# Forward sums of a graph layer as two float32r matmuls, with the message split by ScalarE and VectorE

## The reference, cut to what matters

```
proj = einsum('ni,rio->rno', feat, W)          # 16 relations
m    = proj[etypes, src_idx] + bias
m    = m * (1 / in_degree)[dst_idx][:, None]
out  = segment_sum(m, dst_idx, num_segments=n) # 53125 edges
```

## Time and profile before

| | |
|---|---|
| three runs | 2062.16, 2066.46, 2066.49 us, median 2066.46 |
| profiled execution | span of 2062.0 us from first to last instruction; the lowest run is 0.2 us above it |
| TensorE busy | 1966.0 us, 95% |
| VectorE busy | 1150.2 us, 56% |
| ScalarE busy | 607.9 us, 29% |
| GpSimd busy | 993.8 us, 48% |
| chain that ended last | TensorE 84%, VectorE 5%, DMA 5%, ScalarE 3% |
| line 690, both projections | 733.1 us in 1600 records, two for each matmul |
| line 772, sums of both directions | 486.5 us in 1760 records, two for each matmul |
| line 808, additions | 371.0 us in 880 |
| line 745, gathers | 831.5 us in 832 |

### The profile page before, as it was taken

How to read it: one execution, slowest core, us unless ns; L and a number is a source line. 1 busy time by engine, 2 the same in 40 slices (tenths; PEclk the granted TensorE clock), 3 DMA queues, 4 the chain that set the end, 5 groups by cost and what they waited for, 6 DMA issues and landing times.

```text
span 2062.0 us, 27476 instructions
## 1 busy us (share of the span) xinstructions
PE 1966.0 (95%) x8235; PEld 1360.8 (66%) x8235; DVE 1150.2 (56%) x2484; ACT 607.9 (29%) x1262; POOL 993.8 (48%) x966
## 2 busy tenths in 40 slices
PE   7999999999999999999998889999999499999998
PEld 3446544456666666555565566888888488888897
DVE  4999991056666666444787668555558711111111
ACT  2332333322222222222433222222223722222243
POOL 0000001067777777777567777777762023333332
PEclk9999999999999999999999999999997699999999
DMA  8332235456666656666555454333332754544573
GB/s 293 156 143 98 108 153 229 173 182 196 190 185 191 191 188 193 208 212 206 183 159 175 142 159 139 103 101 102 97 95 82 264 166 113 130 112 122 131 197 73
DMA packets 134186, 326.97 MB, mean 159 GB/s; under 512 B 24576, under 2 KB 65184, under 8 KB 132768
## 3 DMA queue, kind: packets, MB, share of 16 engines
q1 hardware_dynamic: 80064, 199.64, 26.7%
q0 software_dynamic: 50688, 123.79, 23.6%
q10 hardware_dynamic: 3296, 1.80, 0.3%
HBM read 196.42 MB, written 128.71 MB: 158 GB/s over the span
## 4 chain that ended last, share of the span: by engine, by line
PE 84%; DVE 5%; DMA 5%; ACT 3%; issue 2%; POOL 1%; DVEq 0%; POOLq 0%
PE bank L690 31%; PE bank L772 16%; PE bank L1983 10%; PE bank L1994 9%; PE bank L1912 4%; PE bank L1903 4%; DMA arena<-table_bwd,arena 3%; PE bank L597 3%; PE bank L1841 1%; DVE arena L808 1%; POOL arena L745 1%; DVE arena L409 1%; DMA table_fwd<-arena 1%; PE bank L1952 1%; ACT arena L1710 1%
## 5 line engine op out<-in xcount | busy, mean ns | idle before, releaser
L690 PE MATMUL bank<-arena,work 128*128 128x512 f32 x1600 | 733.1, 594 | 2.5 <-ACT arena L683 1.5
L808 DVE TENSOR_TENSOR arena<-arena,bank 128x257 f32 x880 | 371.0, 422 | 370.9 <-PE bank L772 298.8
L772 PE MATMUL bank<-arena 128*128 x1760 | 486.5, 388 | 24.3 <-DMA arena<-table_bwd,arena 15.9
L745 POOL DMA_INDIRECT arena<-table_fwd,arena x416 | 419.9, 1009 | 144.7 <-issue 86.0
L745 POOL DMA_INDIRECT arena<-table_bwd,arena x416 | 411.6, 989 | 152.4 <-issue 81.7
L690 PEld LDWEIGHTS bank<-arena,work 128*128 128x128 f32 x1600 | 299.3, 190 | 278.7 <-issue 261.8
L683 ACT ACTIVATE arena<-bank 128x512 f32<-128x512 f32 x400 | 239.6, 599 | 702.8 <-PE bank L690 699.2
L772 PEld LDWEIGHTS bank<-arena 128*128 128x128 f32 x1760 | 317.1, 191 | 144.0 <-issue 110.0
L1053 POOL DMA_INDIRECT out<-xn,work x56 | 89.5, 1599 | 249.7 <-DVE xn L193 181.7
L754 DVE TENSOR_TENSOR arena<-cst,arena 128x512 f32<-128x512 f32 x220 | 151.5, 689 | 97.9 <-PE bank L690 97.9
L1727 ACT ACTIVATE arena<-bank,work 128x256 f32<-128x256 f32 (+1 forms) x280 | 120.8, 432 | 284.2 <-PE bank L1983 277.6
(11 more groups left out here) (323 smaller groups left out, 1589.5 us busy)
## 6 DMA issues: line engine op xcount, KB each, us to landing
table_fwd<-arena SPq DMA_DIRECT2D x100, 512.0 KB, 2.6
table_bwd<-arena SPq DMA_DIRECT2D x100, 512.0 KB, 3.2
arena<-in_W SPq DMA_DIRECT2D x35, 1024.0 KB, 5.7
arena<-in_W SPq DMA_DIRECT2D x2, 4096.0 KB, 13.9
arena<-table_fwd,arena POOLq DMA_INDIRECT x416, 3.1
arena<-table_bwd,arena POOLq DMA_INDIRECT x416, 2.8
work<-x_transposed SPq DMA_DIRECT2D x50, 128.0 KB, 3.6
mix_rows<-arena SPq DMA_DIRECT2D x25, 256.0 KB, 2.6
```

Source lines behind the costliest of these rows:

```text
L690: last = pe.matmul(ps[4 + s % 2][:, :], xT[t % 2][:, k * P:(k + 1) * P], ar(W_off[d] + k * 4096 + c * 512, 512), start=(k == 0), stop=(k = ...
L745: e.indirect_dma_start(msg[m % RING][:, 0:C], None, table[d], bass.IndirectOffsetOnAxis(ap=idx[d][:, j:j + 1], axis=0)).then_inc(s_ga[m % ...
L772: pe.matmul(ps[sum_bank(n)][:, 0:W], oh[n % OHS], msg_all[:, ds(place.pop(n), W)], start=True, stop=True).then_inc(s_sm, 1)
L808: vec.tensor_tensor(to, to, ps[sum_bank(n)][:, 0:W], ALU.add).then_inc(s_ac, 1)
```

## The change

Each of the 416 forward sums beside the second projection becomes two matmuls in the type float32r. ScalarE copies the message into `hi` (which rounds it to float32r), VectorE subtracts, `lo = message - hi`, and TensorE multiplies the one-hot by `hi` (258 columns, two of them ones) and then by `lo` (256 columns) into the same PSUM bank. There are six buffers for each half. ScalarE works up to four sums ahead of TensorE's slot, VectorE up to two ahead. The 24 forward sums behind the projection and all backward sums stay as they are.

The forward sums now begin at slot 4, not slot 2, and end at slot 197. The halves lie over tiles 12 to 24 of `X1`, so SyncE loads these rows of x again once the last such sum is done, and the first addition to tile 12 waits for that. The one-hots have a tensor of their own. Some semaphores are merged, since new ones are needed. TensorE no longer reads the message's address into registers for these sums; ScalarE and VectorE each do, four addresses at a time.

```diff
+        oh = [onehot[:, j * P:(j + 1) * P] for j in range(OHS)]
+        hi = [half_t[:, j * (C + 2):(j + 1) * (C + 2)] for j in range(HB)]
+        lo = [half_t[:, HB * (C + 2) + j * C:HB * (C + 2) + (j + 1) * C] for j in range(HB)]
...
-            pe.matmul(ps[sum_bank(n)][:, 0:W], oh[n % OHS], msg_all[:, ds(place.pop(n), W)],
-                      start=True, stop=True).then_inc(s_sm, 1)
+            if n in rank:
+                i = rank[n]
+                e.wait_ge(s_lo, i + 1)
+                pe.matmul(ps[sum_bank(n)][:, 0:C + 2], oh[n % OHS], hi[i % HB], start=True, stop=False)
+                pe.matmul(ps[sum_bank(n)][:, 0:C], oh[n % OHS], lo[i % HB], start=False, stop=True).then_inc(s_sm, 1)
+            else:
+                pe.matmul(ps[sum_bank(n)][:, 0:W], oh[n % OHS].bitcast(f32), msg_all[:, ds(place.pop(n), W)],
+                          start=True, stop=True).then_inc(s_sm, 1)
...
+        def high_half(e, n):
+            i = rank[n]
+            if n % 4 == 0:
+                load_halves(act, high_at, n)
+            e.wait_ge(s_ga[n % GS], 16 * (n // GS + 1))
+            if i >= HB:
+                e.wait_ge(s_sm, split[i - HB] + 1)
+            act.activation(hi[i % HB][:, 0:C], msg_all[:, ds(high_at.pop(n), C)], ACT.Copy).then_inc(s_hi, 1)
+        def low_half(e, n):
+            i = rank[n]
+            if n % 4 == 0:
+                load_halves(vec, low_at, n)
+            e.wait_ge(s_hi, i + 1)
+            vec.tensor_tensor(lo[i % HB], msg_all[:, ds(low_at.pop(n), C)], hi[i % HB][:, 0:C],
+                              ALU.subtract).then_inc(s_lo, 1)
...
-            return min(TE - LEFT, max(0, (s - 2) * (TE - LEFT) // (SLOTS - 4)))
+            return min(TE - LEFT, max(0, (s - 4) * (TE - LEFT) // (SLOTS - 6)))
+        def halves_upto(s, ahead):
+            return min(TE - LEFT, forward_upto(s + 1) + ahead) if s >= 4 else 0
+        split = list(range(TE - LEFT))
+        rank = {n: i for i, n in enumerate(split)}
...
+                e.wait_ge(s_sm, split[-1] + 1)
+                e.dma_start(X1[:, XT * C:NT * C].rearrange("p (t c) -> p t c", c=C),
+                            a["x"][XT * P:NT * P, :].rearrange("(t p) c -> p t c", p=P)).then_inc(ldx_again, 16)
...
+                    for n in range(halves_upto(s - 1, 2), halves_upto(s, 2)):
+                        if n in rank:
+                            low_half(e, n)
                     add_sums(e, forward_upto(s), forward_upto(s + 1))
...
                     evacuate(SLOTS + s)
                     late_sort_copies(s)
+                    for n in range(halves_upto(s - 1, 4), halves_upto(s, 4)):
+                        if n in rank:
+                            high_half(e, n)
```

More of the change, by code:

```diff
@@ L28 @@
                             mybir.dt.float16)
+f32r = mybir.dt.float32r
 ALU, ACT, AX = mybir.AluOpType, mybir.ActivationFunctionType, mybir.AxisListType
@@ L138, in end_of_block @@
             nc.all_engine_barrier()
-        arena = sb("arena", 36232)
+        arena = sb("arena", ARENA)
+        with nc.sbuf_tensor("x_lead", [P, XL], f32), nc.sbuf_tensor("halves", [P, HB * (2 * C + 2)], f32r) as half_t:
+            pass
         X1 = sb("X1", NT * C)
+        onehot = sb("onehot", OHS * P, f32r)
         xn = sb("xn", NT * C)
@@ L373, in build @@
         W_off = [R2, R1]
-        ld, lde, ldf, ldh, ldr, zbd = (sem(n) for n in
-            ("ld_const", "ld_edges", "ld_fold", "ld_half", "ld_rows", "zero"))
+        ld, lde, ldf, zbd = (sem(n) for n in
+            ("ld_const", "ld_edges", "ld_fold", "zero"))
         ldx = sems("ld_x", 3)
         XG = ((0, 5), (5, 15), (15, NT))
-        ldw, s_wb = sems("forward_weights", 4), sem("backward_weights")
+        ldw, s_wb = sems("forward_weights", 4), sem("weights_in")
         folded, s_pmo = sem("folded"), sem("fold_out")
@@ L724, in build @@
         msg_ones = ar(R2, RING * W).rearrange("p (j w) -> p j w", w=W)[:, :, C]
-        oh = [ar(R2 + RING * W + j * P, P) for j in range(OHS)]
+        oh = [onehot[:, j * P:(j + 1) * P] for j in range(OHS)]
+        hi = [half_t[:, j * (C + 2):(j + 1) * (C + 2)] for j in range(HB)]
+        hi_ones = half_t[:, 0:HB * (C + 2)].rearrange("p (j w) -> p j w", w=C + 2)[:, :, C:C + 2]
+        lo = [half_t[:, HB * (C + 2) + j * C:HB * (C + 2) + (j + 1) * C] for j in range(HB)]
         msg_all = ar(R2, RING * W)
@@ L789, in load_places, with load_halves @@
             place.update((n + i, v) for i, v in enumerate(at))
+        high_at, low_at = {}, {}
+        def load_halves(eng, at, n):
+            _, v = nc.values_load_multi_w_load_instructions(
+                placei[0][0:1, n:n + 4], engines=(eng.engine,), min_val=0, max_val=(RING - 1) * W,
+                skip_runtime_bounds_check_because="edge_places takes the tile modulo RING before it multiplies by W")
+            at.update((n + i, x) for i, x in enumerate(v) if n + i in rank)
+        def high_half(e, n):
[13 more added lines that the diff above has]
+                              ALU.subtract).then_inc(s_lo, 1)
         def load_columns(n):
@@ L1088, in _ @@
                 e.dma_start(ei[2], a["et"]).then_inc(lde, 16)
-                e.dma_start(so_f.hcst, a["half"]).then_inc(ldh, 16)
+                e.dma_start(so_f.hcst, a["half"]).then_inc(lde, 16)
                 for t in range(NT):
```

55 lines of the change are left out of this document (30 added, 25 removed).

## The result

The changed kernel takes 2095.72 us (median of four executions), the one before 2065.45 beside it: 1.015 times as long, 95% interval 1.0136 to 1.0163, some 30 us. One of the four took 3965.35 us, no trace of it is kept and the ratio leaves it out; the other three lie between 2091.96 and 2097.74, with 2093.70 in the middle. The profiled execution agrees, with a span of 2091.7 us against 2062.0. The forecast was 2075. Its direction was right. The change is between three and four times as large as forecast: inside the range of 8 in 10 (2052 to 2105), outside the forecast's own range (2067 to 2092).

What follows compares the result with a forecast made beforehand. TensorE was taken as the bound, GpSimd and VectorE close behind. Losing 7.3 us in the sort (VectorE) and 0.8 behind it (GpSimd) makes 8 us, so 2075 us; own range 2067 to 2092, 8 in 10 from 2052 to 2105.

Steps and rivals of the forecast that it cites:

- The bound moves to VectorE in the sort: Second projection beside the sort: subtractions add 0.72 us a slot where VectorE had 0.61 to spare, so VectorE becomes the bound.
- The TensorE term: Second projection: 0.24 us a split sum, 0.12 a part; TensorE's slot 2.55 us in the sort, 2.22 behind it.
- Rival 3: Float32r parts in the sums are not cheaper, 0.86 us a sum: 158 us more than forecast, 2233 us; chance 0.04.
- The start: Start of the second projection: slots 0 to 3 run without sums, and VectorE begins its slot 4 at about 425 us.
- VectorE's slot in the sort: Beside the sort: 3.04 us a slot against 2.95, ends 2.98 and 3.23; slot 135 at 823.2, a loss of 7.3 us.
- TensorE does not hold VectorE up: Beside the sort: TensorE may be two sums ahead and low halves are made a slot earlier, so no wait was added.
- The wait for register loads: VectorE's slot in the sort: 0.04 us for one more register load in four sums, 0.18 if all of it is exposed.
- rival 4: TensorE, idle 0.4 us a slot, loses its clock; at 1.2 GHz a tenth of the time: 40 us, 2115; chance 0.05.
- Behind slot 135: Second projection behind the sort: GpSimd is the bound, some 126 gathers left, 170.5 us against 169.7, a loss of 0.8.
- Rival 2: Gathers stretched by VectorE operations with two SBUF inputs, 0.2 us more each: 2128 us, or half of it 2101; chance 0.15.
- Rival 1: Not slower: subtractions fit VectorE's waits in the sort if under 0.29 us with load; GpSimd bounds, 2050 us; chance 0.20.
- The copies on ScalarE: Second projection: 416 copies of 0.42 us each stay hidden, since ScalarE is busy only 22%.

Runs made afterwards that it cites:

- no_low: Changed kernel without the subtraction, TensorE multiplying the high half twice, so sums lack the low part: 2047.51 us, 0.9924 of the kernel before.
- interleaved: Changed kernel with VectorE's order altered: one subtraction between every two additions instead of all subtractions first: 2075.40 us, 1.0051 of the kernel before.
- halves_unused: Changed kernel making and waiting for both halves, but TensorE multiplies the message in float32 as before: 2096.07 us, 1.0160 of the kernel before.
- pe_pad: Changed kernel with the first part of each split sum done once more in front, its result overwritten: 2100.97 us, 1.0181 of the kernel before.
- no_low_once: Changed kernel without the subtraction and without the second matmul part, so sums carry only the rounded message: 2048.77 us, 0.9928 of the kernel before.
- none: Changed kernel with only sum 0 split, keeping later start, one-hots' tensor and second x load, subtractions between additions: 2063.68 us, 1.0002 of the kernel before.
- half: Changed kernel with only the even forward sums split, the odd ones staying float32: 2061.98 us, 0.9995 of the kernel before.
- quarter_sort_i: Changed kernel with only every fourth sum up to slot 135 split, none behind, subtractions between additions: 2057.39 us, 0.9968 of the kernel before.
- late_only: Changed kernel with only the sums from 284 on, behind the sort, split; earlier ones stay float32: 2067.68 us, 1.0020 of the kernel before.
- psum_sub: Changed kernel without low halves or second part, plus an unused subtraction reading PSUM before each addition: 2047.04 us, 0.9929 of the kernel before.

## Why the prediction was right in sign and short in size

**The bound moves to VectorE in the sort: right.** TensorE gaps, VectorE's wait for it near zero, GpSimd late: all as named, though line 696 has 378 records in 300 us and not 395. no_low, interleaved and halves_unused each show it on the chip.

**The TensorE term: somewhat short, right within what mattered.** Two parts behind each other start 0.12 us apart. Timeline of the changed kernel:

```profile
600.79 0.28 PE L785 MATMUL bank<-halves,onehot 128*128 128x258 f32 x1
...
600.91 0.28 PE L786 MATMUL bank<-halves,onehot 128*128 128x256 f32 x1
...
602.10 0.36 PE L785 MATMUL bank<-halves,onehot 128*128 128x258 f32 x1 [0.91 <-DVE halves L832]
602.29 0.28 PE L786 MATMUL bank<-halves,onehot 128*128 128x256 f32 x1
602.41 1.88 PE L696 MATMUL bank<-arena,work 128*128 128x512 f32 x4
```

After a gap the first part takes 0.19. With this and four stretches at the 1.2 GHz level TensorE is busy 263.12/94.5 = 2.78 us a slot and not 2.55, still under VectorE's. Rival 3 (float32r no cheaper) is out.

**The start: right.** The forecast had VectorE's slot 4 at about 425; its first subtraction starts at 425.78.

**VectorE's slot in the sort: the step that failed first.** Forecast 3.04 us, found (836.04 - 425.78)/131 = 3.13, and 3.17 from 500 to 800. The forecast's sum of work was good: without the 7.7 us for TensorE and the 3.2 for ScalarE the slot is (300 - 10.9)/94.5 = 3.06. What was wrong is the sentence "TensorE does not hold VectorE up", and its like for ScalarE: an engine that sets the pace still waits for its neighbours now and then, and a sum of its work is a floor. These waits had been put at nothing, and they are 10.9/94.5 = 0.12 us a slot. Over the 131 slots the slot is 3.13 - 3.04 = 0.09 us longer than forecast, 12 of the 12.8 us that slot 135 is later; the rest is the start, 0.8 later. That is still inside the forecast's own 2.98 to 3.15, so it takes the second step to put the time beyond 2092. The wait for register loads was sized right: 4.1 us of "issue" in front of subtractions in 300, 0.04 a slot.

Most of the 7.7 us come from stretches at the 1.2 GHz level. Here, after a wait of 2.15 us for a low half, a projection lasts 2.77 us and not 1.88:

```profile
535.22 0.36 PE L785 MATMUL bank<-halves,onehot 128*128 128x258 f32 x1 [2.15 <-DVE halves L832]
535.41 0.28 PE L786 MATMUL bank<-halves,onehot 128*128 128x256 f32 x1
535.53 2.77 PE L696 MATMUL bank<-arena,work 128*128 128x512 f32 x4
```

There are seven of 3.4 us beside the second projection, so at most 7 x 1.7 = 12 us of TensorE time; rival 4 had put 40 on the clock. In the 6 or 7 us around each of the four between 500 and 800 us VectorE waits 1.6, 1.0, 1.4 and 0.8 us for TensorE, 4.8 of the 7.7. What share of the 12 reaches the end in the changed kernel stays open: pe_pad did not remove them, and no_low_once shows only that they are free where TensorE has slack.

**Behind slot 135: the step that failed second.** Forecast 170.5 us, found 178.0. The last gather starts 1005.06 - 836.04 = 169.0 us behind slot 135 (forecast 163.5 - 1.3 = 162.2) and the end follows 9.0 us later (forecast 8.3). Of the 6.8 us of the gathers, 3.9 are three more than assumed: 287 have been issued by then, so 129 are left, not 126. The rest is not the pitch. From 844.24 on 125 gathers start within 160.8 us, one in 1.297, and 1.298 was forecast. It is a stall of GpSimd just behind slot 135, which the forecast did not have:

```profile
839.84 0.36 PE L785 MATMUL bank<-halves,onehot 128*128 128x258 f32 x1 [3.96 <-DVE halves L832]
840.04 0.31 PE L786 MATMUL bank<-halves,onehot 128*128 128x256 f32 x1
840.16 3.57 PE L696 MATMUL bank<-arena,work 128*128 128x512 f32 x4
...
840.62 0.94 POOL L755 DMA_INDIRECT arena<-table_fwd,arena  x1 [0.92 <-PE bank L786]
844.24 0.95 POOL L755 DMA_INDIRECT arena<-table_fwd,arena  x1 [2.68 <-PE bank L786]
```

While VectorE writes out the places, it makes no low halves, and TensorE stands for 3.96 us. The projection behind that wait lasts 3.57 us and not 1.88, since the granted clock is 0.50, the 1.2 GHz level, from 840.2 to 843.6. Two gathers wait 0.92 and 2.68 us for a sum where 0.30 is the rule, 3.0 us more. So here the low clock probably reaches the end, with up to the 1.7 us of the projection; no run shows it by itself.

The gathers behind it, and those of before from 820 to 975 us:

```profile
L755 POOL DMA_INDIRECT arena<-table_fwd,arena x121 | 120.2, 993 | 39.9 <-issue 27.4 <-PE bank L786 12.4
```
```profile
L745 POOL DMA_INDIRECT arena<-table_fwd,arena x122 | 119.2, 977 | 37.2 <-issue 26.8 <-PE bank L772 10.4
```

The first row is from 840 to 1000 us, so its idle time holds the 2.68. The gathers are 16 ns longer each, half of the 0.03 us that was allowed. The table shows more: every variant with high halves behind slot 135 takes 173.5 us or more there, even without a subtraction, and none takes 171.9. Two things add up in it. A kernel that is early at slot 135 has more gathers left: 127 in before, 128 in none, 130 in half and quarter_sort_i, 132 in no_low. And from the start of the last gather to the end it takes 7.5 us in before, 7.6 in none and 7.5 in quarter_sort_i, 8.1 in no_low, 9.0 in the changed kernel and 9.2 in late_only. A message goes through ScalarE, and through VectorE, before TensorE may sum it, which is the likely reason.

The two steps make 12.8 + 7.5 us. With 1.3 us behind the second projection they are the 21.6 us by which 29.7 exceeds the 8.1 of the forecast.

**Rival 2: real, and too small to carry the loss.** The gathers are stretched by operations with two SBUF inputs and not by those that read PSUM, as the timeline rows of before let one suspect. The 100 gathers that start within a subtraction make 10 us, 0.024 a gather over all 416, where the forecast had 0.03. The rival's 0.2 us a gather supposed that a gather waits out a train of operations; it waits for one. Beside a VectorE that sets the pace GpSimd has waits in which this can hide; how much of the 10 us hides there is not shown. The Trainium skill ("SBUF — State Buffer", SBUF: two separate sides) has the port pair held for the whole instruction while the other engine is blocked. The trace agrees: the gather's record ends later by what is left of the one instruction, less 0.13 us.

**Rival 1: its bound was right.** It put the best case, GpSimd at its floor, at 2050; no_low and psum_sub give 2047. It failed on its own condition, 0.29 us for a subtraction with its load. Two subtractions in a row start 0.34 us apart (median).

**The rest.** The copies on ScalarE cost nothing that can be seen in no_low; in the changed kernel VectorE waits 3.2 us in 300 for them. The second load of x and the late start of the sums cost nothing that can be seen (none).

## What to carry to other kernels

Before making an engine's work cheaper, count what the other engines of the same loop have left: here TensorE was 100% busy and its saving of 79 us (416 x 0.19) was worth at most 16, because GpSimd was 5% behind it and VectorE 20%. Where a change moves the bound to another engine, a sum of that engine's work is the floor of the new loop, and waits for its neighbours (0.12 us in 3.17 here) come on top. A place where the new bound does a long piece of other work, like slot 135 here, wants a look of its own. On a full VectorE it matters where new work stands. Put into the gap of a dependent pair, 416 subtractions that read PSUM and that nobody waits for cost nothing. The real ones, which others wait for, cost some 47 us in a block and some 26 interleaved, against the same kernel without them.

## What the runs showed of the hardware that was not expected

- A float32r part of 256 or 258 columns takes 0.12 us from start to start when it follows another, and 0.19 as the first after a gap, against 0.43 for one float32 matmul of 257 columns.
- Reading four addresses into registers takes 344 ns in the median and up to 1205 ns on a busy VectorE:

```profile
L811 DVEq TENSOR_LOAD <-work x104: 336/344/1205, 417.9 to 1004.6; - x104
L811 ACTq TENSOR_LOAD <-work x104: 304/309/1161, 424.2 to 1004.0; - x104
```

- In the changed kernel, where TensorE was busy 88% from 500 to 800 us, its granted clock fell to the 1.2 GHz level seven times beside the second projection, for 3.4 us each, each time within 1.3 us of the end of a gap of 1.7 to 4.0 us. Before, it did so once there, at 423.2 us, with the wait of 2.95 us for the first gather.
- A gather that starts while VectorE runs an operation with two SBUF inputs ends later by what is left of that operation, less 0.13 us. One that starts beside an operation with a PSUM input lasts 947 ns, as beside an idle VectorE.
